# Linear attention's per-tile order of VectorE, ScalarE and TensorE, expert biases added by VectorE, and deferred semaphore release

## What is computed

```
x = x + linear_attention(layernorm(x))
      # K = h as 16 heads of 16; Q, V = rms_norm(h Wq^T), rms_norm(h Wv^T) per head, times weights
      # W_t = sum over s <= t of K_s (x) V_s ;  out_t = Q_t W_t
x = x + moe0(layernorm(x))      # 16 experts, 2 per token
      # gu = t Wgu + bgu ; gate = min(gate, 7) ; up = clip(up, -7, 7)
      # hid = (up + 1) * gate * sigmoid(1.702 gate) ; y = hid Wd + bd ; weighted sum over the 2
x = x + softmax_attention(layernorm(x))   # 16 heads of 64, low-rank q, k, v, rotary positions
x = x + moe1(layernorm(x))      # 64 experts, 8 per token, capacity 64
```

## Time and profile before

| | us |
|---|---|
| median of 3 runs | 4507.91 (4502.37 to 4509.51) |
| the profiled execution, its own time | 4506.27 |
| its span, first to last instruction | 4504.5 |
| linear attention | 0 to 437.1 |
| first experts | 437.1 to 777.8 |
| the stages behind them | 777.8 to 4504.5 |

### The profile page before, as it was taken

How to read it: one execution, slowest core, us unless ns; L and a number is a source line. 1 busy time by engine, 2 the same in 40 slices (tenths; PEclk the granted TensorE clock), 3 DMA queues, 4 the chain that set the end, 5 groups by cost and what they waited for, 6 DMA issues and landing times. The chain is left out here.

```text
span 4504.5 us, 54711 instructions
## 1 busy us (share of the span) xinstructions
PE 3984.1 (88%) x17866; PEld 3005.5 (67%) x17866; DVE 3574.9 (79%) x4436; ACT 2646.0 (59%) x3555; POOL 2209.0 (49%) x1837
## 2 busy tenths in 40 slices
PE   6774998683999999999999999999999999989563
PEld 3443554452788888888888888888888888867421
DVE  4454443774899999999999999999999999956611
ACT  4442333331677777777777777777777777742221
POOL 1234665464455555555555555555555555530154
PEclk8776999786999999999999999999999999989776
DMA  6001333666222232223222322232223223137296
GB/s 242 20 22 39 56 61 59 221 217 185 63 53 57 49 81 50 57 49 81 53 53 49 81 55 53 57 76 56 51 58 72 56 51 64 34 113 235 74 243 165
DMA packets 349678, 384.04 MB, mean 85 GB/s; under 512 B 141532, under 2 KB 279585, under 8 KB 336851
## 3 DMA queue, kind: packets, MB, share of 16 engines
q1 hardware_dynamic: 325334, 354.22, 30.8%
q0 software_dynamic: 24064, 26.32, 3.5%
HBM read 232.55 MB, written 117.84 MB: 78 GB/s over the span
## 5 line engine op out<-in xcount | busy, mean ns | idle before, releaser
L1523 POOL TENSOR_TENSOR at_pl<-at_pf,at_ph 128x512 fp32r<-128x512 f32 x1024 | 1330.0, 1299 | 1343.0 <-ACT at_ph L1670 1342.7
L1669 ACT ACTIVATE at_pf<-at_ps_s 128x1024 f32<-128x1024 f32 x1024 | 1051.0, 1026 | 747.5 <-PE at_ps_s L1719 747.5
L1586 DVE TENSOR_TENSOR at_pl<-at_pf,at_ph 128x512 fp32r<-128x512 f32 x1024 | 1355.4, 1324 | 20.6 <-ACT at_ph L1670 20.6
L1568 DVE TENSOR_REDUCE at_mx<-at_ps_u 128x2 f32<-128x1024 f32 x1024 | 1250.2, 1221 | 24.5 <-PE at_ps_u L1703 24.4
L1670 ACT ACTIVATE at_ph<-at_ps_s 128x1024 fp32r<-128x1024 f32 x1024 | 1042.7, 1018 | 0.0
L1719 PE MATMUL at_ps_s<-at_q,at_k 66*128 66x512 f32 x2048 | 820.7, 401 | 0.0
L1718 PE MATMUL at_ps_s<-at_q,at_k 128*128 128x512 f32 x2048 | 812.2, 397 | 0.3 <-ACT at_ph L1670 0.3
L1735 PE MATMUL at_ps_v<-at_ph,at_vh 128*128 128x512 f32 x2048 | 810.1, 396 | 0.2 <-POOL at_pl L1523 0.2
L1737 PE MATMUL at_ps_v<-at_pl,at_vh 128*128 128x512 f32 x2048 | 809.5, 395 | 0.0
L1736 PE MATMUL at_ps_v<-at_ph,at_vl 128*128 128x512 f32 x2048 | 809.2, 395 | 0.0
L1703 PE MATMUL at_ps_u<-at_k,at_qp 128*128 128x512 f32 x2048 | 648.0, 398 | 63.5 <-DMA at_q<-at_low 47.7
(11 more groups left out here) (254 smaller groups left out, 4116.1 us busy)
## 6 DMA issues: line engine op xcount, KB each, us to landing
at_k<-kT SPq DMA_DIRECT2D x64, 512.0 KB, 10.0
at_q<-qT SPq DMA_DIRECT2D x64, 512.0 KB, 9.3
wgu<-Wgu_in SPq DMA_DIRECT2D x64, 384.0 KB, 5.2
qT<-pj_rot SPq DMA_DIRECT2D x32, 512.0 KB, 3.1
vT<-pj_vo SPq DMA_DIRECT2D x32, 512.0 KB, 4.4
kT<-pj_rot SPq DMA_DIRECT2D x32, 512.0 KB, 3.1
at_raw<-qT SPq DMA_DIRECT2D x32, 512.0 KB, 4.7
at_raw<-kT SPq DMA_DIRECT2D x32, 512.0 KB, 6.6
```

The costliest lines, as they stand in the source:

```text
L1523: pool.tensor_tensor(pl[:, n % NP, at], pf[:, n % NP, at], ph[:, n % NP, at].bitcast(F32), ALU.subtract).then_inc(s["pl2_ready"], 1)
L1568: dve.tensor_reduce(mx[:, qb % 2, 2 * i:2 * i + 2], ps_u[:], X, ALU.max).then_inc(s["u_max"], 1)
L1586: dve.tensor_tensor(pl[:, n % NP, at], pf[:, n % NP, at], ph[:, n % NP, at].bitcast(F32), ALU.subtract)\
L1669: act.activation(pf[:, n % NP], ps_s[:, n % 2], ACT.Exp, scale=DH ** -0.5)
```

## The change

- **TensorE's turn**: `logits` and `positions`, with their waits for `xa_ready`, `lg_ready` and `pos_read`, move from the head of the turn to behind `outputs_T(i)`.
- **VectorE's turn**: `measure(i+12)`, `squares_sum(i+4)` and `roots(i+4)` move to the head, ahead of `masked(i+1)`; `logits` and `counted` stand between them; `update(i)` and `measure(i)` follow `masked`.
- **ScalarE's turn**: `tokens(i+6)` and `roots(i+4)` move ahead of `outputs(i)`, `routed_T(i-7)` to the end. `queries` writes its unscaled copy in one 128x256 instruction instead of two scaled 128x128 ones; the scale is folded into the block mask (`blocksw`, one new VectorE product at the start).
- **Late routed tiles**: for odd tiles from 28 on the transpose goes to the PSUM of q and v, which is idle by then.
- **Biases**: only the down bias (256 values an expert) is still split in three parts; it is loaded at the start, split in turn -7 and stored at once. Two waits are new: ScalarE's `squares(0)` waits for the split, VectorE waits in turn -1 for the store's landing. Gate and up biases are read from DRAM with one row broadcast to 128 partitions, 16 DMAs, into the SBUF of x, two experts behind each stored quarter.
- **Experts**: `gate_up` loses its bias product. VectorE loads the expert's number into a register of its own, adds the broadcast bias to gate and up (128x512, from PSUM) into a new buffer `gu`, and clips from there.
- **Semaphores**: `release` runs after `project` and after `add_odd` instead of after each stage.

```diff
+            blocksw = sb("blocksw", [P, DC, P])
...
@@ SyncE
+                sp.dma_start(bsrc, ins["bd"]).then_inc(s["biases"], 16)
                 for q in range(1, Q):
                     load_x(q)
...
+                sp.wait_ge(s["bias_split"], 5)
+                sp.dma_start(self.bias_dram[:].rearrange("k e n -> e k n"), bpart).then_inc(s["bias_out"], 16)
                 sp.wait_ge(s["zero_ready"], 1)
...
+                def load_bias(q):
+                    sp.wait_ge(s["x_out"], 16 * (q + 1))
+                    for e in (2 * q, 2 * q + 1):
+                        sp.dma_start(self.bgu0[:, e], ins["bgu"][e].partition_broadcast(P)).then_inc(s["experts_in"], 16)
...
-                    if q == Q - 2:
-                        sp.wait_ge(s["a_ready"], 4 * NT)
-                        sp.dma_start(bsrc[:, 0:2 * F0], ins["bgu"]).then_inc(s["biases"], 16)
-                        sp.dma_start(bsrc[:, 2 * F0:], ins["bd"]).then_inc(s["biases"], 16)
-                sp.wait_ge(s["bias_split"], 5)
-                sp.dma_start(self.bias_dram[:].rearrange("k e n -> e k n"), bpart).then_inc(s["bias_out"], 16)
+                    load_bias(q)
@@ VectorE
                 for i in range(FIRST, END):
                     j = i - 8
-                    if tile(j) and j % 4 == 3:
-                        logits(j // 4)
-                    if tile(j - 1) and (j - 1) % 4 == 3:
-                        counted((j - 1) // 4)
...
-                    if tile(i + 1):
-                        masked(i + 1)
-                    if tile(i + 4):
-                        squares_sum(i + 4)
-                    if tile(i):
-                        update(i)
-                        measure(i, (s["xa_ready"], i + 1), mv2, s["mv2_ready"])
-                    if tile(i + 4):
-                        roots(i + 4)
+                    if i == -7:
+                        split_biases()
+                    if i == -1:
+                        dve.wait_ge(s["bias_out"], 16)
                     t = i + 12
                     if tile(t) and t > 3:
                         measure(t, (s[f"x{t // 4}"], 16), mv1, s["mv1_ready"])
+                    if tile(i + 4):
+                        squares_sum(i + 4)
+                        roots(i + 4)
+                    if tile(j) and j % 4 == 3:
+                        logits(j // 4)
+                    if tile(j - 1) and (j - 1) % 4 == 3:
+                        counted((j - 1) // 4)
+                    if tile(i + 1):
+                        masked(i + 1)
+                    if tile(i):
+                        update(i)
+                    if tile(i):
+                        measure(i, (s["xa_ready"], i + 1), mv2, s["mv2_ready"])
@@ ScalarE
-                    if tile(i):
-                        outputs(i)
-                    if tile(i - 7):
-                        routed_T(i - 7)
-                    if tile(i + 4):
-                        roots(i + 4)
-                    if tile(i + 6):
-                        tokens(i + 6)
+                    if tile(i + 6):
+                        tokens(i + 6)
+                    if tile(i + 4):
+                        roots(i + 4)
+                    if tile(i):
+                        outputs(i)
...
                     if tile(i - 6):
                         routed(i - 6)
+                    if tile(i - 7):
+                        routed_T(i - 7)
@@ TensorE
-                    (logits(j), positions((j - 1) // 4) and their waits, at the head of the turn)
...
                     if tile(i):
                         outputs_T(i)
+                    if tile(j):
+                        if i > 0:
+                            pe.wait_ge(s["xa_ready"], min(i, NT))
...
+                        logits(j)
+                    if tile(j - 1) and (j - 1) % 4 == 3:
...
+                        positions((j - 1) // 4)
                     if tile(i + 1):
                         scores(i + 1)
@@ experts, TensorE and VectorE
-                        pe.wait_ge(s["gate_ready"], i - 1)
-                        pe.wait_ge(s["up_ready"], i - 1)
-                    pe.matmul(out, self.ones_bf[0:3, :], bias[:, bass.ds(e, 1), 0:2 * F].squeeze(1),
-                              start=True, stop=False)
+                        pe.wait_ge(s["gu_ready"], i - 1)
...
+                def clipped(i):
+                    e = dve.value_load(self.tile_expert[0:1, 0, i:i + 1], min_val=0, max_val=E0 - 1)
+                    dve.wait_ge(s["g_ready"], i + 1)
...
+                    dve.tensor_tensor(gu[:, i % 2], ps_g[:, i % 2], self.bgu0[:, bass.ds(e, 1)].squeeze(1), ALU.add)\
+                        .then_inc(s["gu_ready"], 1)
...
+                    dve.wait_ge(s["gu_ready"], i + 1)
+                    dve.tensor_scalar(gate[:, i % 2], gu[:, i % 2, 0:F], 7.0, None, ALU.min).then_inc(s["gate_ready"], 1)
+                    dve.tensor_scalar(up[:, i % 2], gu[:, i % 2, F:], 7.0, -7.0, ALU.min, ALU.max).then_inc(s["up_ready"], 1)
```

More of the change, by code:

```diff
@@ L143, in __init__ @@
         self.nc, self.ins, self.out = nc, ins, out
-        self.sems = 0
+        self.held = []
     def build(self):
@@ L193, in scope, with release @@
         ps = lambda name, shape, dt=F32: ctx.enter_context(nc.psum_tensor(f"{stage}_{name}", shape, dt))
-        held = []
         def sem(name):
[L197 to L204, removed]
+            self.held.append(nc.alloc_semaphore(f"{stage}_{name}"))
+            return self.held[-1]
         return ctx, sb, ps, sem
+    def release(self):
+        self.nc.clear_and_free_semaphores(self.held)
+        self.nc.all_engine_barrier()
+        self.held = []
     def linear_attention(self):
@@ L278, in linear_attention @@
             block = ctx.enter_context(nc.Block())
-            BW = 2 * F0 + D
-            bsrc, brest = (buf[0:E].rearrange("p a b -> p (a b)")[:, 0:BW] for buf in (xnT, sq))
-            bpart = at[0:E].rearrange("p h l -> p (h l)")[:, 0:3 * BW // 2].bitcast(BF16).rearrange("p (k n) -> p k n", k=3)
+            BW = D
+            room = at[0:E].rearrange("p h l -> p (h l)")
+            bsrc, brest = room[:, 0:BW], sq[0:E].rearrange("p a b -> p (a b)")[:, 0:BW]
+            bpart = room[:, BW:BW + 3 * BW // 2].bitcast(BF16).rearrange("p (k n) -> p k n", k=3)
             below, begin = (buf.rearrange(f"p {a} -> p ({a})")[:, 0:(ST0 + 1) * E].rearrange("p (n e) -> p n e", e=E)
@@ L298, in sums, with routed_at @@
                 return (TB - 2) * (t // TB) + max(0, min(t % TB, LAST) - 1)
+            def routed_at(t):
+                return ps_qv[:, 0:D] if t >= NT - 4 and t % 2 else ps_t[:, 0]
             vn3 = vn[:].rearrange("p r g t d -> p r (g t d)")
@@ L462, in update @@
                         dst = state[:, (t + 1) % 2] if t % TB == 0 else kvm[:, t % 2]
-                        dve.tensor_tensor(dst, ps_k[:, 1], blocks.unsqueeze(1).broadcast_to([P, DC, P]), ALU.mult)\
+                        dve.tensor_tensor(dst, ps_k[:, 1], blocksw[:], ALU.mult)\
                             .then_inc(s["kvm_ready"], 1)
@@ L512, in split_biases @@
                 def split_biases():
-                    dve.wait_ge(s["biases"], 32)
-                    dve.wait_ge(s["oT_ready"], NT)
+                    dve.wait_ge(s["biases"], 16)
                     part = Chain(dve, s["bias_split"])
@@ L795, in _ @@
                     j = i - 8
-                    if tile(j):
-                        if i > 0:
-                            pe.wait_ge(s["xa_ready"], min(i, NT))
-                        if j >= 4 and j % 4 == 0:
-                            pe.wait_ge(s["lg_ready"], j // 4)
-                        if j >= 5 and j % 4 == 1:
-                            pe.wait_ge(s["pos_read"], j // 4)
-                        logits(j)
-                    if tile(j - 1) and (j - 1) % 4 == 3:
-                        pe.wait_ge(s["xa_ready"], min(i, NT))
-                        pe.wait_ge(s["lg_ready"], (j - 1) // 4 + 1)
-                        positions((j - 1) // 4)
                     if tile(i + 2) or tile(i + 5):
@@ L823, in _ @@
                         outputs_T(i)
+                    if tile(j):
+                        if i > 0:
+                            pe.wait_ge(s["xa_ready"], min(i, NT))
+                        if j >= 4 and j % 4 == 0:
+                            pe.wait_ge(s["lg_ready"], j // 4)
+                        if j >= 5 and j % 4 == 1:
+                            pe.wait_ge(s["pos_read"], j // 4)
+                        logits(j)
+                    if tile(j - 1) and (j - 1) % 4 == 3:
+                        pe.wait_ge(s["xa_ready"], min(i, NT))
+                        pe.wait_ge(s["lg_ready"], (j - 1) // 4 + 1)
+                        positions((j - 1) // 4)
                     if tile(i + 1):
@@ L830, in _ @@
                             pe.wait_ge(s["q_ready"], i + 3)
-                        if tile(i - 8):
+                        if i - 7 >= NT - 2:
```

(10 more changed lines are left out.)

40 lines of the change are left out of this document (25 added, 15 removed).

## The result

The changed kernel takes 4353.52 us (median of 4 runs, 4351.00 to 4355.53) against 4506.09 (4 runs, 4502.37 to 4509.51): ratio 0.9665, 95% interval 0.9652 to 0.9677, some 153 us faster. The forecast was 4338.0 with a range of 4312 to 4392. The two profiled spans are 4504.5 and 4353.7 us, 150.8 apart.

What follows compares the result with a forecast made beforehand. Linear attention was bound by a ring of waits between engines, the experts by TensorE's work. Savings of 125.8, 5.0, 6.0, 4.9, 24.5 and 4.0 sum to 170.2 us off 4506.3, giving 4338 us for the median; range 4312 to 4392.

Steps and rivals of the forecast that it cites:

- The turns: Linear attention, tiles 0 to 27: reordered turns take 6.2 us without a router, 7.0 with one; 125.8 us saved.
- half clock stays: Linear attention: project remains at 3.37 us although the idle is gone; 30 us more, 4368 us; chance 0.20.
- The ring closes elsewhere: Linear attention: transposes wait for ScalarE's late routed_T, held by VectorE's sum; 46 us more, 4384 us; chance 0.15.
- the 6.61 of the sum: Linear attention: TensorE's own work in one turn at full clock, 6.61 us.
- the step that described the ring: Linear attention: scores, mask, sum, x, logits, project, outputs, scores form a 10.85 us loop; TensorE idles 2.75 us before logits.
- Start: Start of linear attention: two turns no longer mask before the sum of squares, four have tokens before roots; 6.0 us saved.
- Turns 28 to 31: Linear attention, turns 29 to 31: no project to hide the mask, so their loop hardly shortens; nothing saved.
- End: End of linear attention: bias DMA wait and split vanish, but GpSimd's scatters become the limit; 4.9 us saved, not 6.3.
- Experts: Experts' stage: removing TensorE's bias product saves 0.31 us on each of 79 tiles, 24.5 us; VectorE's addition is hidden.
- experts gain nothing: Experts' stage: GpSimd becomes the bound by sharing SBUF interfaces with VectorE, tile stays 3.93 us; 4362 us; chance 0.06.
- Release: Semaphore clearing barriers after stages: seven become two, 5 x 0.8 = 4.0 us saved.

Runs made afterwards that it cites:

- the run with both: Changed kernel, experts: VectorE's bias addition kept, and a TensorE bias product (3 rows by 512 columns, wrong rows) put back ahead of the weights' product; 4363.59 us.
- neither bias step: Changed kernel with neither TensorE's bias product nor VectorE's bias addition in the experts, so gate and up biases are left out; 4341.50 us.

## Why the prediction was right, and where it was not

**The turns** (125.8 forecast, 119.0 measured). 6.46 us in the first seven against 6.2, 7.25 in the twenty with a router against 7.0. The clock came back as argued: project at 1.88 us in each turn, 1.00 over the window, and *half clock stays* fell. What the Trainium skill says on frequent short idles (TensorE: Matmul & The Clock Gate, "A second HAM failure mode") did not come true here: TensorE still has some 8.5 us of idles in that window, and the clock holds. *The ring closes elsewhere* stays small: in three of the 20 turns the transposes wait 0.9 to 1.1 us for ScalarE's copy of the routed tile (turns of 7.7 and 7.8 instead of 7.1), and in the first five TensorE waits 0.55 us for GpSimd's addition of the state. TensorE's own work is 6.8 us a turn (136.47 / 20), 0.2 above the 6.61 of the sum.

But **the step that described the ring was half of the story**. I wrote that the wait for x ahead of the logits held back transposes and `project`, "which need nothing of it", and priced VectorE's and ScalarE's moves only by waits that they add, 1.0 us. The early turns of before, 10.2 us long without any logits, already spoke against that. I used their 1.88 us for project, which is from the first turns, and did not ask why those behind them took 10.2. With my reasons alone, TensorE's move would have given nearly all; by itself it gives 27 us, 14.5 of them in its stage. The sum came out because the change opens both rings, which the prediction did not see: the size of this term is right partly by luck.

**Start** (6.0, measured 9.7). VectorE's and ScalarE's order is worth 12.4 us here (34.9 us to tile 0's update against 47.3 with all orders old), twice what was forecast, and the rest of the change, put at nothing, costs 2.7. Which part of it does was not tried; that the second ring makes the 12.4 fits, and was not followed step by step.

**Turns 28 to 31** (nothing forecast, 4.0 lost). From 28 to 30 TensorE's clock is 1.00 before and 0.70 after. What the turn to 28 gained (3.9) is lost there. But the two turns take 13.8 to 18.7 us in kernels that are alike in them, so the 4.0 is not shown to be the change's.

**End** (4.9 gained forecast, 7.2 lost). The bias stall is gone and that was right: VectorE has no splitting there. The term failed in its step from the stall to GpSimd's scatters: the last eight wait for the last quarter, GpSimd idle 9.20 us ahead of them, where before 4.86 us stood ahead of the last 16, and the last quarter waits for the late copies. On the chip without late copies the tail was 46.7 to 48.0, still not 48.6 - 4.9 = 43.7.

**Experts** (24.5, measured 28.9, of which 26.5 lie between the first gate product and the last). The total is near for two errors against each other. The removed product freed 0.51 us a tile, as the run with both shows, while I had measured only from its start to the next product's. Against it stands what I had put at nothing, GpSimd: at 3.44 it is level with TensorE's 3.42, and the long tiles take back some two fifths. That is *experts gain nothing* in mild form, though by the gathers' landing and not by sharing a port. On the latter: by the Trainium skill, GPSIMD Engine Reference, Specifications, GpSimd's SBUF interfaces are shared with VectorE, with contention when VectorE runs in a 2-port mode or has two SBUF inputs. The profile does not show in which mode the clips ran. The gather is 1.11 us in the changed kernel against 1.04 before and with neither bias step, which agrees; with both steps it is 1.04 although clips and addition run as in the changed kernel, which does not. The chip is not the reason: on the chip of these two runs the one with ScalarE alone old, whose experts are the changed ones, has 1.11. No run tells more.

**Release** (4.0). Where a release was taken out, its time is gone: before, 1.2 us pass from the end of GpSimd's drain behind the last scatter (430.6, 5.3 us long) to the first instruction of the experts, 0.2 after (309.9, 5.3 us long). At this place the drain also began 0.8 us later behind the scatter, so the stretch shows only 0.2. The five lasted 0.8, 0.6, 0.6, 0.9 and 0.6 us before, 3.5 in all. What the sum left out is that the two that remain clear more semaphores and last longer, 1.3 and 1.2 us instead of 0.5 and 0.3 (drain and last event of SyncE, kernel after):

```profile
L206 SPq DRAIN  x2: 7/7/7, 922.2 to 4352.5; - x2
...
L206 SPq EVENT_SEMAPHORE  x2: 17/17/17, 923.5 to 4353.7; - x2
```

That leaves some 1.8 us of the 4.0, an estimate from these marks. The stages behind can't confirm it: they differ by 0.2 us here, and among the traces with the same code there they range from 3716.7 to 3729.2. No run put the releases back alone.

## What to carry to other kernels

Before pricing a reorder, look for every ring through the busiest step, and look at stretches where the one you suspect cannot act: here turns without logits. The engines' orders belong together: in the stage, TensorE's move alone gave 14 us, ScalarE's on top of it cost 29, VectorE's and ScalarE's without it gave 58, all together 131. And compare stage by stage with the untouched stages in view: two times here pointed to the wrong theory by 8 us and more that lay in stages the edit did not touch, and half of what TensorE's move seems to give by the time lies there too.

## What the runs showed of the hardware

In the long tails the engine that waits for TensorE starts late: for transposes issued at 281.00 and lasting 0.67 us, ScalarE's copy of them started at 286.66 (the run without broadcasts), at a clock of 0.50, with 6 GB/s of traffic between 279 and 288. The half clock alone does not make it: the run with both biases has 0.50 between 272 and 286 and no late copy. It happens in the same three places of the program in all seven traces of changed code on two of the three chips that the record names, and in none of the four on the third; the broadcasts, the second bank, the order of the last turns and the three engines' orders are ruled out as its only cause. Whether TensorE finished late or its signal came late, the traces don't tell, since the ends of matmuls are modelled.
